# Carries and shifted copies of a two-branch attention kernel: made on ScalarE, or by transfers on SyncE's queue

## What is computed

```python
x = L0_attn_x
xn = _layernorm(x, axis=-1)
x = x + _L0_attn_ref(xn, ...) + _L0_ffn_ref(xn, ...)

# one layer of _L0_ffn_ref (two of them, 8 heads of 64, windows of 64 tokens)
def shift_token(t):
    t1, t2 = jnp.split(t, 2, axis=-1)
    t2 = jnp.pad(t2, ((0, 0), (1, 0), (0, 0)))[:, :-1]
    return jnp.concatenate([t1, t2], axis=-1)
h = shift_token(x)
q, k, v = jnp.split(h @ wqkv, 3, axis=-1)
q, k = rotary_xpos(l2norm(q) * qs, l2norm(k) * ksc)
# each window of 64 queries sees its own 64 keys and the 64 before them
bk, bv = look_around(bk), look_around(bv)
attn = softmax(where(mask, -max, einsum('bhwid,bhwjd->bhwij', bq, bk)))
x = x + einsum('bhwij,bhwjd->bhwid', attn, bv) @ wo
h = layernorm(shift_token(x)) * lg + lb
a, g = split(h @ w1 + b1, 2, axis=-1)
x = x + (a * gelu(g)) @ w2 + b2
```

## Time and profile before

| what | value |
|---|---|
| time, median of 3 runs | 972.21 us (970.54 to 973.97) |
| span of the profiled execution, first to last instruction | 969.5 us |
| PE busy | 862.3 us (89%) |
| ACT busy | 701.7 us (72%) |
| DVE busy | 634.5 us (65%) |
| POOL busy | 631.0 us (65%) |
| granted clock of TensorE, mean | 0.983 |
| 16 DMA engines, mean rate | 14 GB/s |

### The profile page before, as it was taken

The page is one execution under the profiler, slowest core; times in us unless marked ns, Lnnn a source line. Parts: engine busy times, 40 slices in busy tenths (PEclk is TensorE's granted clock), DMA queues, the critical chain, the costliest instruction groups (busy, mean ns, idle before and its releaser), DMA issues.

```text
span 969.5 us, 26414 instructions
## 1 busy us (share of the span) xinstructions
PE 862.3 (89%) x10836; PEld 580.5 (60%) x10836; DVE 634.5 (65%) x1082; ACT 701.7 (72%) x1449; POOL 631.0 (65%) x500
## 2 busy tenths in 40 slices
PE   0678889989899898998999989999999999999876
PEld 0345666666667666666566656565656565656552
DVE  5874666666667567576575776757575758575632
ACT  0446786977868779677797778787878787878651
POOL 4588677675876758667586665757575758585700
PEclk9979999999999999999999999999999999999997
DMA  9100000000000000000000000000000000000000
GB/s 295 30 1 3 1 2 2 3 3 2 2 3 1 3 1 1 3 2 3 1 2 3 1 2 2 1 21 4 17 7 23 2 23 2 21 3 24 1 23 11
DMA packets 20482, 13.47 MB, mean 14 GB/s; under 512 B 4579, under 2 KB 19597, under 8 KB 20237
## 3 DMA queue, kind: packets, MB, share of 16 engines
q1 hardware_dynamic: 15108, 10.49, 3.6%
q10 hardware_dynamic: 5256, 1.31, 0.7%
HBM read 9.70 MB, written 2.10 MB: 12 GB/s over the span
## 4 chain that ended last, share of the span: by engine, by line
PE 63%; ACT 15%; DVE 10%; issue 7%; POOL 3%; DMA 1%; DVEq 0%; POOLq 0%; SPq 0%; ACTq 0%
PE pQK L1181 8%; PE pS L1108 6%; PE pT L1093 5%; PE pT L1050 5%; PE pM L1125 5%; PE pV L1146 4%; PE pS L1082 4%; PE pM L1254 4%; DVE m L734 4%; PE pT L1237 3%; PE pQK L1345 3%; PE pM L1119 2%; PE pS L1069 2%; ACT prT L545 2%; ACT pr L598 1%
## 5 line engine op out<-in xcount | busy, mean ns | idle before, releaser
L366 POOL TENSOR_TENSOR rn<-rn,half_neg 128x16 f32<-128x16 f32 x64 | 187.5, 2929 | 5.3
L379 POOL TENSOR_TENSOR m<-m 128x1024 f32<-128x1024 f32 x64 | 150.9, 2358 | 0.0
L364 POOL TENSOR_SCALAR rn<-ss 128x16 f32<-128x16 f32 x64 | 16.3, 254 | 193.3 <-DVE ss L747 192.1
L386 POOL TENSOR_TENSOR qkn<-m,rn 128x1024 f32<-128x1024 f32 x64 | 121.7, 1902 | 5.0
L1181 PE MATMUL pQK<-wqkv,hT 128*128 128x512 f32 x256 | 123.6, 606 | 0.9 <-DVE m L734 0.9
L780 DVE TENSOR_REDUCE mx<-pS 128x8 f32<-128x1024 f32 x64 | 78.1, 1220 | 63.8 <-PE pS L1082 63.8
L561 ACT ACTIVATE sq<-pQK 128x1024 f32<-128x1024 f32 x64 | 65.4, 1022 | 25.5 <-PE pQK L1181 25.4
L747 DVE TENSOR_REDUCE ss<-sq 128x16 f32<-128x1024 f32 x64 | 77.6, 1213 | 6.7 <-ACT sq L561 6.4
L782 DVE TENSOR_TENSOR pr<-pS,mx 128x1024 f32<-128x1024 f32 x64 | 78.4, 1225 | 2.2
L521 ACT ACTIVATE kT<-pT 128x512 f32<-128x512 f32 x64 | 38.0, 595 | 57.3 <-PE pT L1050 56.8
L545 ACT ACTIVATE prT<-pT 128x1024 f32<-128x1024 f32 x64 | 65.0, 1016 | 15.6 <-PE pT L1093 14.8
(11 more groups left out here) (169 smaller groups left out, 2015.9 us busy)
## 6 DMA issues: line engine op xcount, KB each, us to landing
x<-in_L_attn_x SPq DMA_DIRECT2D x4, 512.0 KB, 9.4
xs<-in_L_attn_x SPq DMA_DIRECT2D x8, 256.0 KB, 2.8
out<-aqkT SPq DMA_DIRECT2D x8, 256.0 KB, 2.2
wqkv<-in_L_ffn_wqkv SPq DMA_DIRECT2D x2, 768.0 KB, 9.8
tab<-in_k_tab SPq DMA_DIRECT2D x1, 1024.0 KB, 10.4
w<-in_L_ffn_w SPq DMA_DIRECT2D x2, 341.0 KB, 10.5
wo<-in_L_ffn_wo SPq DMA_DIRECT2D x2, 256.0 KB
cst<-in_k_cst ACTq DMA_DIRECT2D x1, 404.5 KB, 4.3
```

The source lines that it names most:

```text
L366: eng.tensor_tensor(rn[:, k % 2, :], rn[:, k % 2, :], half_neg[:, 0:2 * H], ALU.pow).then_inc(S["rn_done"], 1)
L379: eng.tensor_tensor(m1[:, k % 2, :], m1[:, k % 2, :], m2[:, :], ALU.add).then_inc(S["add_done"], 1)
L386: eng.tensor_tensor(qkn[:, k % 2, :].rearrange("p (h d) -> p h d", d=DH), m1[:, k % 2, :].rearrange("p (h d) -> p h d", d=DH), rn[:, k % 2 ...
```

## The change

All five kinds of copies above leave ACT and become transfers that SP starts: the keys' carry, the values' carry (upper half of `vmix`), the lower half of `vmix` (now copied from `vown` after its eviction, since a transfer can't read the projection's bank), and the two halves of the shifted input. SP gets a program of its own, `sp_slot`, written out slot by slot for all bodies; the loads of `xs` and the stores of `out` stand in it in slots 0 and 2. The shifted input of a sequence is fetched a whole body ahead, as soon as the projection of this step has read the old one. Each kind gets one semaphore for each sequence, and the waits on ACT and PE change accordingly: `vown`'s eviction waits for the transfer of the upper half (`v_kept`), `kT`'s eviction for the keys' carry of a body earlier (`k_kept`), the value projection for `h_ld`, and `pe_values` for `v_top` beside `v_ev`.

```diff
+        def sp_shift(sp, step, b):
+
+            src = xnT if step[0] == 0 else x2T
+            for rows, back in ((slice(0, 64), 0), (slice(64, P), 1)):
+                col0 = step[1] * P + 1 - back
+                sp.dma_start(hT[rows, b, :], src[rows, b, col0:col0 + P]).then_inc(h_ld[b], 16)
+
+        def sp_slot(sp, new, old, ff, k):
+            S = LS
+            output = ff[1] if ff and ff[0] == 1 else None
+            if k == 0 and output:
+
+                sp.wait_ge(G["out"], 16 * output)
+                sp.dma_start(xs[:, :, :], x_steps[output]).then_inc(G["xs"], 16)
+            if new and not is_start(new):
+
+                sp.wait_ge(S["o_mm"], count(new, k) - 3)
+                sp.dma_start(vmix[k][64:P, :, 0:DH], vown[k][64:P, :, 0:DH]).then_inc(v_kept[k], 16)
+            if k == 2 and output is not None:
+                sp.wait_ge(G["osb"], output + 1)
+                sp.dma_start(out_steps[output], osb[:, :, :]).then_inc(G["out"], 16)
+            if new:
+
+                sp.wait_ge(S["v_ev"], count(new, k) + 1)
+                sp.dma_start(vmix[k][0:64, :, 0:DH], vown[k][0:64, :, 0:DH]).then_inc(v_top[k], 16)
+            turned = at(new, old, k - 2)
+            if turned and next_step(turned[0]):
+
+                step, b, m = turned
+                sp.wait_ge(S["s_mm"], m + 1)
+                sp.dma_start(kT[b][:, :, P:P + WIN], kT[b][:, :, WIN:P]).then_inc(k_kept[b], 16)
+            if new and next_step(new):
+
+                after = next_step(new)
+                sp.wait_ge(S["qk_mm"], count(new, k) + 1)
+                if after[0] == 1:
+                    sp.wait_ge(S["x2_done"], after[1] + 1)
+                sp_shift(sp, after, k)
...
+            sp.wait_ge(memset_done, 7 + 4 * NB)
+            sp.wait_ge(xnt_ev, 1)
+            for b in range(NB):
+                sp_shift(sp, (0, 0), b)
             sp.dma_start(xs[:, :, :], x_steps[0]).then_inc(G["xs"], 16)
...
         def act_slot(eng, new, old, ff, k):
             S = LS
             if new:
                 n = count(new, k)
-                if k == 0:
-                    if new[0] == 1:
-                        eng.wait_ge(S["x2_done"], new[1] + 1)
-                    act_shift(eng, new, 0)
...
                 eng.wait_ge(S["t_mm"], 2 * m + 1)
                 if not is_start(step):
-                    eng.wait_ge(S["carried"], m - 3)
+                    eng.wait_ge(k_kept[b], 16 * step_count(step))
...
             if new:
-                if not is_start(new):
-
-                    need(eng, S["o_mm"], n - 3)
-                    eng.activation(vmix[k][64:P, :, 0:DH], vown[k][64:P, :, 0:DH], ACT.Copy).then_inc(S["v_kept"], 1)
-                    eng.activation(kT[k][:, :, P:P + WIN], kT[k][:, :, WIN:P], ACT.Copy).then_inc(S["carried"], 1)
-                if k < NB - 1:
-                    act_shift(eng, new, k + 1)
-
                 eng.wait_ge(S["v_mm"], n + 1)
                 if not is_start(new):
-                    eng.wait_ge(S["v_kept"], n - 3)
-                values = pV[:, :].rearrange("p (h d) -> p h d", h=H)
-                eng.activation(vown[k][:, :, 0:DH], values, ACT.Copy).then_inc(S["v_ev"], 1)
-                eng.activation(vmix[k][0:64, :, 0:DH], values[0:64], ACT.Copy).then_inc(S["v_ev"], 1)
+                    eng.wait_ge(v_kept[k], 16 * step_count(new))
+                eng.activation(vown[k][:, :, 0:DH], pV[:, :].rearrange("p (h d) -> p h d", h=H), ACT.Copy).then_inc(S["v_ev"], 1)
...
             eng.wait_ge(S["pt_ev"], n + 1)
-            eng.wait_ge(S["v_ev"], 2 * n + 2)
+            eng.wait_ge(S["v_ev"], n + 1)
+            eng.wait_ge(v_top[b], 16 * (n // NB) + 16)
...
-                eng.wait_ge(S["h_ready"], 2 * n + 2)
-                need(eng, S["v_ev"], 2 * n)
+                eng.wait_ge(h_ld[k], 32 * step_count(new) + 32)
+                need(eng, S["v_ev"], n)
```

More of the change, by code:

```diff
@@ L238, in program @@
         LS = {n: sem(n) for n in (
-            "carried", "v_kept", "h_ready", "qk_mm", "v_mm", "sq_done", "ss_done", "mul_done", "max_ss", "rn_done", "add_done",
+            "qk_mm", "v_mm", "sq_done", "ss_done", "mul_done", "max_ss", "rn_done", "add_done",
             "qkn_done", "t_mm", "t_ev", "v_ev", "s_mm", "mx_done", "sub_done", "exp_done",
@@ L243, in program @@
             "hf_done", "w2_mm", "x2_done")}
+        h_ld = [sem(f"h_ld{b}") for b in range(NB)]
+        v_top = [sem(f"v_top{b}") for b in range(NB)]
+        v_kept = [sem(f"v_kept{b}") for b in range(NB)]
+        k_kept = [sem(f"k_kept{b}") for b in range(NB)]
         A = {n: sem(f"a_{n}") for n in (
@@ L303, in run_bodies, with next_step @@
             body(None, None, (1, NT - 1))
+        def next_step(step):
+            if step[1] + 1 < NT:
+                return (step[0], step[1] + 1)
+            return (1, 0) if step[0] == 0 else None
+        def sp_shift(sp, step, b):
[29 more added lines that the diff above has]
+                sp_shift(sp, after, k)
         @block.sync
@@ L318, in _, with body @@
                 sp.dma_start(w2[0:CHUNKS[2][1], l, 2, :], a["L0_ffn_w2"][l, 2 * P:HID, :]).then_inc(w_ld, 16)
+            sp.wait_ge(memset_done, 7 + 4 * NB)
+            sp.wait_ge(xnt_ev, 1)
+            for b in range(NB):
+                sp_shift(sp, (0, 0), b)
             sp.dma_start(xs[:, :, :], x_steps[0]).then_inc(G["xs"], 16)
[L321 to L327, removed]
+            sp.wait_ge(xnt_ev, NT)
+            def body(new, old, ff):
+                for k in range(NB):
+                    sp_slot(sp, new, old, ff, k)
+            run_bodies(sp, body)
             sp.wait_ge(G["out"], 16 * NT)
@@ L493, in act_load_table @@
             eng.activation(warm[:, place:place + 1], half_neg[:, 0:1], function)
[L495 to L501, removed]
         def act_slot(eng, new, old, ff, k):
@@ L1261, in pe_retention_project @@
                 eng.wait_ge(A["xa"], 4 * t + 4)
-                eng.wait_ge(LS["v_ev"], 2 * (4 * t + 4))
+                eng.wait_ge(LS["v_ev"], 4 * t + 4)
             need(eng, A["qk"], 2 * (n - 1))
```

## The result

The changed kernel takes 964.0 us, median of 4 runs (961.0 to 965.1), against 972.0 us before (median of 4 runs on the same chip, 970.5 to 974.0). The ratio is 0.9913, with a 95% interval from 0.9896 to 0.9929. The profiled execution spans 961.9 us, before 969.5 us. So 8.0 us are gained where 7.2 were forecast, and the forecast of 965.0 us with its range from 961 to 973 holds.

What follows compares the result with a forecast made beforehand. PE was taken to hold 63% of the chain of waits, with ACT's copies on it in only eight places. Block slots 6.7 plus start 0.5 give 7.2 us off 972.2: 965.0 us, range 961 to 973.

Steps and rivals of the forecast that it cites:

- Block slots: Seven slots of layer 1: ACT's copies make PE wait for oT, 0.95 us each; the whole stall goes, 6.7 us.
- The start: First value projection: shifts become transfers, so PE starts some 0.13 us after the last xnT eviction; 0.5 us less.
- The upper half of `vmix`: Tight in slots 2 and 3: the transfer takes 2.5 us, has 1.5 us of cover, and nothing is charged.
- The threshold: Ordinary slot: vown's eviction has 4.1 us after the values are through, 4.0 us of it for the transfer.
- Rival A: Upper half of vmix lands beyond 4.0 us, and each microsecond more comes back on PE 30 times; chance 0.14.
- there is nothing between: Slots 2 and 3, 30 times: no product between the previous slot's values and this slot's need of the transfer.
- Transfers as a whole: 312 transfers: 37 ns a piece, a quarter of the span on each DMA engine, 0.39 us SP issue; no limit.
- Small pieces: 256-byte pieces inside SBUF: if a piece doubled to 74 ns, the transfer would take 3.7 us, still under 4.0.
- The price beyond the threshold: Slots 2 and 3: each microsecond of transfer time beyond 4.0 us comes back on PE 30 times.
- B: Block slots: half the stall stays if the transfer lands late or the silus are paced later; 968.3 us, chance 0.15.
- C: Stretches such as after slot 3: ACT's freed 138 us gain some 3.5 us more; 961.5 us, chance 0.05.

Runs made afterwards that it cites:

- e1: Changed kernel, but the 35 copies in layer 1's seven block slots stay on ACT and the other 277 are transfers: 971.49 us, ratio 0.9990.
- e6: Changed kernel, but SP starts and waits for one small 32 KB transfer ahead of each upper half of vmix: 984.38 us, ratio 1.0106.
- e7: Changed kernel, but SP starts and waits for two small 32 KB transfers ahead of each upper half of vmix: 1075.62 us, ratio 1.1030.

## Why the prediction was right

- **Block slots.** Taken as 7 x 0.95 = 6.7 us; measured 6.74 us from the value projections, and undoing just them (e1) gives back all but 0.5 us of 8. The steps within the slot hold on the old slot's scale, which lies 2.11 us later: vown at 733.73 (733.7 taken), the silus at 734.59 and 735.44 (734.5 and 735.4), their end at 736.13 (736.1), oT's end at 739.19 (739.2). The 0.4 us by which oT should be early is 0.44.
- **The start.** 0.5 us taken. The changed kernel there, ACT and then PE:

```profile
40.22 0.60 ACT L740 ACTIVATE xnT<-pV 128x512 f32 x1 [0.91 <-PE pV L1404]
```

```profile
41.02 2.04 PE L1178 MATMUL pV<-wqkv,hT 128*128 128x512 f32 x2 [0.94 <-issue]
```

  PE starts 41.02 - 40.82 = 0.20 us after the last xnT, before 41.74 - 41.08 = 0.66 us: 0.46 us. Another 0.26 us is that xnT itself came earlier. The prediction counts this term in full, as a chain to the end; that isn't shown. The lead of 0.72 us is gone at the fifth value projection, and in time it can't be measured: e1 keeps the start and is 0.5 us under before, within the interval.
- **The upper half of `vmix`.** 2.5 us taken between bounds of 2.0 and 4.0. By its line, 60 transfers (issue on SP in ns, then issue to landing):

```profile
L333 SPq DMA_DIRECT2D vmix<-vown x60: 590/616/1187, 76.1 to 890.5; - x60
...
DMA to landing us min/median/max: 2.5/2.6/3.7
```

  The threshold, taken as 4.0 us from the landing's side and 4.1 us for vown's start, measured about 4.3 us (e6). Rival A was thus 1.5 us away, and with one turn more on SP it came true: e6 is slower than before. The prediction's "there is nothing between" holds for slots 3 and for slots 2 of layer 0, not for slots 2 of layer 1 (4.7 us); and in slots 3 of layer 0 the delay reaches PE by the product into pV and not through prT and oT.
- **Transfers as a whole.** Here two sizes were off, without consequence. A piece was taken at 37 ns, the mean of a queue with other loads; with 18.0% of 16 engines over 961.9 us for 122,500 packets it is 22.6 ns, and DMA's share 18% where a quarter was expected. SP's issue was taken at 0.39 us from the load of `xs`; for these transfers it is 0.6 us, five of them 3 us in a slot and not 2.0. It isn't a matter of the kind of transfer alone, since the issue of the same load is longer in the changed kernel:

```profile
L329 SPq DMA_DIRECT2D xs<-in_L_attn_x x7: 368/586/971, 661.1 to 931.0; - x7
```

  Both had cover.
- **Small pieces.** The Trainium skill ("DMA: Bandwidth & Descriptors", Specifications) has pieces under 512 bytes read, modified and written. The same page of the Trainium skill, in its section "Why small descriptors are slow (HBM only)", leaves transfers inside SBUF out of the penalty, so it speaks against these transfers less than the prediction has it. The prediction's estimate, with the time of a piece doubled, was 3.7 us for the transfer. With 256-byte pieces inside SBUF the median is 2.6 us, so no such doubling shows here.
- **The price beyond the threshold.** Taken as 30 us for each microsecond, from slots 2 and 3 alone. The second turn of 1.73 us cost 91 us, 53 for each. PE's busy time in e6, then in e7:

```profile
PE 864.0 (88%) x10836; PEld 578.2 (59%) x10836; DVE 634.3 (65%) x1082; ACT 572.5 (58%) x1137; POOL 631.2 (64%) x500
```

```profile
PE 892.5 (83%) x10836; PEld 593.7 (55%) x10836; DVE 635.3 (59%) x1082; ACT 569.0 (53%) x1137; POOL 631.0 (59%) x500
```

  Of the spans of 982.5 and 1075.0 us, PE is idle for 118.5 and 182.5 us: 64 us more, or 37 for each. The term was too small even so: ahead of the drain PE waits for oT 34 times in e7, 13 of them in slots 1, against 19 times and once in e6. The other 28.5 us are busy time of PE. They come with a lower mean clock, 0.966 in e7 against 0.985 in e6, but that they are the clock's alone isn't shown: at nearly the same mean clock as the changed kernel (0.984), e6 has 7.0 us more busy time.
- **The 0.8 us that the forecast lacks** lies inside the interval of the measurement (6.9 to 10.1 us of gain). The spans differ by 7.6 us, of which 6.7 are the block slots. The rest is what is left of 0.8 us ahead of the switch, 1.6 lost there and 1.6 gained in the drain. So the mechanism of the large term is shown. That the whole sum comes within 1 us of the measured time is partly luck: the start's 0.5 us isn't shown to last, and changes of 1.6 us that have nothing to do with the edit happened to cancel in the profiled pair.

Rivals B and C are out: no part of the stall is left in the block slots, and C's 3.5 us more lie beyond what e1's interval leaves for the 277 copies elsewhere (2.5 us).

## What to carry to other kernels

A busy engine that the chain of waits names in a few slots only is worth relieving in those slots only: 35 of 312 copies carried the gain, and one group of copies, the carries, would have done. Work out how far ahead the consumer would be if the copy went, since what is taken beyond that is not gained. Where a copy becomes a transfer, count the time from the release of its source to the first need of its target and compare it with issue to landing: here it was 2.75 us of 4.3, and one small transfer more to wait for turned the gain into a loss.

## What the runs showed of the hardware that was not expected

In the changed kernel a transfer inside SBUF of 128 KB in 512 pieces of 256 bytes lands 2.6 us after its issue (median of the upper halves; 2.9 of the lower), one of 32 KB in 64 pieces 1.8 us: four times the bytes take some 1 us more. Its issue takes SP 0.6 us; a load of 256 KB from HBM took 0.38 us of SP before and 0.59 in the changed kernel (medians of 7), so a price read from one place of a queue need not hold at another. In e6 6 of 60 such transfers came some 1.6 us late with no cause that the profile shows. And the granted clock, at two places of a few tens of microseconds, moved single executions by some 1.6 us either way, as much as a fifth of what this change is worth.
